# Softmax row sums of the long query chunks: from TensorE products with ones to sums on VectorE and one product per chunk

## The reference, cut to what matters

```python
paths = sigmoid(x @ Wp + bp)                       # 8 heads x 5 per token
agree = pq * pk + (1.0 - pq) * (1.0 - pk)
sim   = cumprod(agree, -1).sum(-1) / 5             # [head, query, key]
sim   = where(key > query, -inf, sim)
attn  = softmax(sim, -1)                           # exp / row sum over the keys
ctx   = attn @ V
x = layernorm(x + ctx @ Wo)
x = layernorm(x + (silu(x @ wg.T) * (x @ wu.T)) @ wd.T)
```

## Time and profile before

| | us |
|---|---|
| median of 3 runs | 887.72 (886.24 to 887.82) |
| the profiled execution, its own time | 885.52 |
| its span, first to last instruction | 883.8 |
| mean granted TensorE clock | 0.98 of full |

### The profile page before, as it was taken

The page is one execution under the profiler, slowest core; times in us unless marked ns, Lnnn a source line. Parts: engine busy times, 40 slices in busy tenths (PEclk is TensorE's granted clock), DMA queues, the critical chain, the costliest instruction groups (busy, mean ns, idle before and its releaser), DMA issues.

```text
span 883.8 us, 15437 instructions
## 1 busy us (share of the span) xinstructions
PE 832.1 (94%) x6146; PEld 412.3 (47%) x6146; DVE 481.5 (54%) x1021; ACT 454.1 (51%) x721; POOL 233.2 (26%) x266
## 2 busy tenths in 40 slices
PE   5299999999999999999999999999999999899986
PEld 3144355453644546454554536445364545344353
DVE  2934437645566545645376455665456553754466
ACT  2146654656456563656545564565636555364522
POOL 0011132223313232231322233132421313232224
PEclk9599999999999999999999999999999999999998
DMA  6750535005520336105360055303370062500001
GB/s 228 203 127 4 119 83 158 1 25 120 143 97 1 80 78 179 48 1 143 75 166 1 17 128 134 106 1 76 72 187 2 1 143 56 137 1 1 24 1 50
DMA packets 44362, 71.09 MB, mean 80 GB/s; under 512 B 3584, under 2 KB 21248, under 8 KB 44288
## 3 DMA queue, kind: packets, MB, share of 16 engines
q1 hardware_dynamic: 44288, 70.07, 30.1%
HBM read 53.28 MB, written 16.78 MB: 79 GB/s over the span
## 4 chain that ended last, share of the span: by engine, by line
PE 87%; DVE 6%; issue 2%; DMA 2%; ACT 1%; POOL 1%; SPq 1%; POOLq 0%; DVEq 0%; ACTq 0%
PE misc L821 17%; PE ctx_ps L786 16%; PE slot L764 15%; PE den_ps L786 13%; PE misc L833 9%; PE misc L740 7%; PE misc L798 6%; PE misc L749 2%; ACT probs L449 1%; DVE x1T_lo L600 1%; DMA query_stack<-phi_dram 1%; PE slot L821 1%; DVE ctx_raw L520 1%; PE misc L807 1%; DMA bp_sb<-in_bp_dram 1%
## 5 line engine op out<-in xcount | busy, mean ns | idle before, releaser
L449 ACT ACTIVATE probs<-slot 128x1024 f32<-128x1024 f32 (+3 forms) x384 | 290.1, 808 | 338.9 <-PE slot L764 338.6
L764 PE MATMUL slot<-query_stack,key_stack 128*128 128x512 f16 (+3 forms) x768 | 161.1, 331 | 16.3 <-DMA query_stack<-phi_dram 15.0
L786 PE MATMUL ctx_ps<-probs,vz_sb 128*32 128x512 f32 (+3 forms) x1536 | 164.5, 500 | 5.2 <-DVE ctx_raw L520 3.8
L402 POOL TENSOR_TENSOR work<-work 128x512 f16<-128x512 f32 x96 | 117.8, 1227 | 184.1 <-ACT work L467 184.1
L786 PE MATMUL den_ps<-probs,ones 128*32 128x512 f32 (+3 forms) x1536 | 159.6, 487 | 0.0
L388 POOL TENSOR_SCALAR_AFFINE_SELECT probs<-probs 128x512 f32<-128x512 f32 x128 | 82.0, 643 | 287.5 <-ACT probs L449 286.5
L821 PE MATMUL misc<-x1T_hi,w_parts 128*128 128x512 f16 x358 | 135.6, 379 | 6.3 <-DVE x1T_lo L600 6.0
L821 PE MATMUL misc<-x1T_lo,w_parts 128*128 128x512 f16 x358 | 135.7, 379 | 0.0
L610 DVE SCALAR_TENSOR_TENSOR work<-work,misc 128x512 f32<-128x512 f32 x89 | 61.1, 686 | 135.0 <-ACT work L461 135.0
L764 PEld LDWEIGHTS slot<-query_stack,key_stack 128*128 128x128 f16 x768 | 56.4, 98 | 167.5 <-issue 117.6
L833 PE MATMUL misc<-w_parts,work 128*128 128x256 bf16 x720 | 85.4, 276 | 3.9 <-POOL work L402 3.9
(11 more groups left out here) (74 smaller groups left out, 668.8 us busy)
## 6 DMA issues: line engine op xcount, KB each, us to landing
key_stack<-phi_dram SPq DMA_DIRECT2D x64, 256.0 KB, 5.7
query_stack<-phi_dram SPq DMA_DIRECT2D x64, 256.0 KB, 6.3
xT_sb<-in_xT_dram SPq DMA_DIRECT2D x8, 1024.0 KB, 5.0
x_sb<-in_x_dram SPq DMA_DIRECT2D x8, 1024.0 KB, 5.6
out_dram<-x SPq DMA_DIRECT2D x15, 512.0 KB, 3.5
phi_dram<-phi_hi SPq DMA_DIRECT2D x16, 256.0 KB, 2.1
phi_dram<-phi_lo SPq DMA_DIRECT2D x16, 256.0 KB, 2.4
work<-in_wgT_dram SPq DMA_DIRECT2D x1, 768.0 KB, 7.9
```

The source lines that it names most:

```text
L402: pool.tensor_tensor(hid_lo[:, n % M1, :], hid[:, n % HSLOTS, :], hid_hi[:, n % M1, :], ALU.subtract).then_inc(hid_lo_ready, 1)
L449: act.activation(probs[:, s % P_SLOTS, 2 * p:2 * p + 2, off:CH], slot[p][:, :, off:CH], ACT.Exp).then_inc(slot_drained[p], 1)
L764: mm = pe.matmul(slot[p][:, k, off:CH], key_stack[:, h, P * j:P * (j + 1)], query_stack[:, h, CH * c + off:CH * (c + 1)], start=True, stop ...
L786: mm = pe.matmul(sums[32 * k:32 * k + 32, off:CH], w, probs[:, s % P_SLOTS, k, off:CH], start=first, stop=final)
```

## The change

`ADD_FROM = {2: 3, 3: 1}`: in chunk 2 the steps of key tile 3 and later, in chunk 3 those of key tile 1 and later, are `ADDED`; those that come after the first of them are `ADDS`. In an added step `weigh` leaves out its four products with ones. In their place a new VectorE task `sum`, in the plan one step after the probabilities are made and ahead of that step's `BETWEEN` tasks, adds the four heads' probabilities (up to 128 x 2048, float32) into a new buffer `acc`; the first of a chunk adds two steps' probabilities. After the chunk's last `weigh`, four products of ones with `acc` go to `den_ps`. Five steps of chunk 2 (four adds) and seven of chunk 3 (six adds) are concerned. ScalarE waits for the add (`summed`) before it writes a ring buffer again, VectorE's `normalise` waits for `acc_used`.

```diff
+    ADD_FROM = {2: 3, 3: 1}
+    ADDED = [i for i, (q, c, g, j) in enumerate(STEPS) if q in ADD_FROM and j >= ADD_FROM[q]]
+    ADDS = [i for i in ADDED if STEPS[i][3] > ADD_FROM[STEPS[i][0]]]
+    NA = len(ADD_FROM)
...
-        return ([("weigh", b, NS - 3)] + gate_pair(b, 2) + [("weigh", b, NS - 2), ("weigh", b, NS - 1)] + halves(b, 2)
+        return ([("sum", b, NS - 1), ("weigh", b, NS - 3)] + gate_pair(b, 2) + [("weigh", b, NS - 2), ("weigh", b, NS - 1)] + halves(b, 2)
...
+        if s >= 1 and (s - 1) % NS in ADDS and s <= B * NS:
+            plan += [("sum", *divmod(s - 1, NS))]
         plan += between(b, i)
...
+        acc = sb("acc", [P, 4, CH], F32)
...
                 if s >= P_SLOTS:
                     act.wait_ge(pv_done, s - P_SLOTS + 1)
+                    b2, i2 = divmod(s - P_SLOTS, NS)
+                    if i2 in ADDED:
+
+                        i2 += i2 not in ADDS
+                        act.wait_ge(summed, len(ADDS) * b2 + ADDS.index(i2) + 1)
...
+            def add_up(b, i):
+
+                q, c, g, j = STEPS[i]
+                off = max(P * j - CH * c, 0)
+                s = NS * b + i
+                own = probs[:, s % P_SLOTS, :, off:CH]
+                count = len(ADDS) * b + ADDS.index(i)
+                if i in DIAG:
+                    dve.wait_ge(masked, len(DIAG) * b + DIAG.index(i) + 1)
+                else:
+                    for p in range(2):
+                        dve.wait_ge(slot_drained[p], s + 1)
+                if j == ADD_FROM[q] + 1:
+                    used = NA * b + list(ADD_FROM).index(q)
+                    if used:
+                        dve.wait_ge(acc_used, used)
+                    dve.tensor_tensor(acc[:, :, :], probs[:, (s - 1) % P_SLOTS, :, :], own, ALU.add).then_inc(summed, 1)
+                else:
+                    dve.wait_ge(summed, count)
+                    dve.tensor_tensor(acc[:, :, off:CH], acc[:, :, off:CH], own, ALU.add).then_inc(summed, 1)
...
                 dve.wait_ge(pv_done, NS * b + LAST[q] + 1)
+                if q in ADD_FROM:
+                    dve.wait_ge(acc_used, NA * b + list(ADD_FROM).index(q) + 1)
...
-                for sums, taken in ((ctx_ps, ctx_out), (den_ps, den_out)):
+                if first and NQ * b + q >= 1:
+                    pe.wait_ge(ctx_out, NQ * b + q)
+                for k in range(4):
+                    h = 4 * g + k
+                    mm = pe.matmul(ctx_ps[32 * k:32 * k + 32, off:CH], vz_sb[:, b % 2, j, 32 * h:32 * h + 32],
+                                   probs[:, s % P_SLOTS, k, off:CH], start=first, stop=final)
+                if i not in ADDED:
                     if first and NQ * b + q >= 1:
-                        pe.wait_ge(taken, NQ * b + q)
+                        pe.wait_ge(den_out, NQ * b + q)
                     for k in range(4):
-                        h = 4 * g + k
-                        w = vz_sb[:, b % 2, j, 32 * h:32 * h + 32] if taken is ctx_out else ones[:, :]
-                        mm = pe.matmul(sums[32 * k:32 * k + 32, off:CH], w,
+                        mm = pe.matmul(den_ps[32 * k:32 * k + 32, off:CH], ones[:, :],
                                        probs[:, s % P_SLOTS, k, off:CH], start=first, stop=final)
                 mm.then_inc(pv_done, 1)
+                if i in ADDED and final:
+                    pe.wait_ge(summed, len(ADDS) * b + ADDS.index(i) + 1)
+                    for k in range(4):
+                        mm = pe.matmul(den_ps[32 * k:32 * k + 32, :], ones[:, :], acc[:, k, :], start=False, stop=True)
+                    mm.then_inc(acc_used, 1)
```

More of the change, by code:

```diff
@@ L273, in seq_postln_kernel @@
         den_out = sem("den_out")
+        summed = sem("summed")
+        acc_used = sem("acc_used")
         den_recip_ready = sem("den_recip_ready")
@@ L695, in _ @@
                     split_weights()
+                elif what == "sum":
+                    add_up(*n)
                 elif what == "normalise":
```

## The result

| | before | after |
|---|---|---|
| median, us | 887.68 (886.24 to 887.82, 4 runs) | 862.49 (861.99 to 864.53, 4 runs) |
| ratio | | 0.972, 95% interval 0.9701 to 0.9739 |
| profiled execution, us | 885.52 | 864.53 |
| its span, us | 883.8 | 862.8 |
| a batch, us | 103.29 | 100.18 |

Faster by 25 us where 16 were forecast (872, range 850 to 885). The time lies inside the range, but 1.5 us under the forecast's own bounds (864 to 882). A second series of runs, beside the kernel before on the same chip, gave 862.31 and a ratio of 0.9739 (0.9717 to 0.9761), so 23 to 25 us. The two profiled executions differ by 21.0, because before's lies 2.2 under its median and after's 2.0 over it.

What follows compares the result with a forecast made beforehand. TensorE's work was taken as the bound. Per batch, 0.4 us (steps 13 to 15) plus 2.3 (19 to 23) minus 0.4 (the rest) gave 2.3, seven times 16: 869.5 profiled, 872 us median, range 850 to 885.

Steps and rivals of the forecast that it cites:

- The sum: Whole kernel: 2.3 us saved a batch, seven times, 16 us, giving a median of 872 us.
- the first rival: GpSimd's masks and subtracts hardly exclude VectorE's adds: 4.1 us saved a batch, about 858 us; chance 0.21.
- The bound and the removal: TensorE's work binds; leaving out products with ones takes 0.88 us off a 512-query step, net 6.2 us a batch.
- The adds: VectorE's new adds: 2.27 us for 2048 elements, 16.5 us a batch, VectorE busy about 613 us.
- The gate steps: Steps 19 to 23: add, mask and subtract take turns; 17.9 us after 20.19, saving 2.3 of 4.2 us.
- Steps 13 to 15: Chunk 2: TensorE waits about 2 us for a buffer behind VectorE's adds; 0.4 of 2.4 us stays saved.
- blocked mask: Steps 13 to 15: perhaps 0.6 us for a mask, counted in VectorE's 7.8 to 8.4 us.
- Steps 16, 17, 0 and 1: Steps 16 and 0 save 0.45 us each, 17 and 1 gain 0.88 less 0.23: together 0.4 us lost.
- The last batch: Chunk 3 saves nothing there, since TensorE's projection starts 0.26 us after the last `normalise`.
- The ring: ScalarE's wait before rewriting a probability buffer costs nothing as long as VectorE lags by less than a step.
- The slower rival: VectorE's queue in steps 19 to 23 and 13 to 14: nothing overlaps, 5.5 us a step, about 912 us; chance 0.16.
- The signs: Products with ones fall about 63 us; adds over 3 us behind mask or subtract; L402 and L388 well above 1.23 and 0.64.

Runs made afterwards that it cites:

- nearly no adds: The changed kernel with every add cut to the last 32 queries of each head: 841.99 us, ratio 0.9488.
- where GpSimd only writes: The changed kernel with GpSimd's mask and subtract replaced by constant writes, so GpSimd reads nothing in SBUF: 855.71 us, ratio 0.9644.
- chunk 3 alone: The change in chunk 3 only, with chunk 2 as in the kernel before: 871.89 us, ratio 0.9832 to the kernel before.
- all-late kernel: The changed kernel with every add moved behind the other VectorE tasks of its plan step: 901.47 us, ratio 1.016.
- two late kernels: The changed kernel with every add behind its plan step's other tasks, with three probability ring buffers (901.47 us) and with four (861.22 us).

## Why the prediction was right, and where it was off

The direction, the mechanism and the places of the waits were right; the sum was 9.5 us too slow. The forecast's own bounds (864 to 882) were missed by 1.5 us, and the range held because it took in the first rival as well.

- **The bound and the removal: right, a little too high.** 6.2 us a batch were counted from starts 0.88 us apart; four products are worth 0.85, and with nearly no adds 5.4 us arrive.
- **The adds: right.** 2.27 us estimated, 2.28 measured alone; VectorE 614 us busy for 613 to 615.
- **The gate steps: a mis-sized term.** "In a diagonal step (20 to 23) add, mask and subtract in turn are 2.27 + 0.64 + 1.16 = 4.07 us" led to 11.5 us for steps 20 to 22. They take 3.84 + 3.58 + 3.78 = 11.2, and 17.5 instead of 17.9 for steps 19 to 23. From one add's start to the next it is 3.58 and 3.78 us (509.50, 513.08, 516.86), because whole durations were added. A VectorE instruction begins 0.07 to 0.08 us before the one ahead has ended (add at 509.50, next at 511.71: 2.21 for 2.29), and mask and subtract together stick out over L648 and L656 by only 0.3 us. The rule that the prediction cites from the Trainium skill (SBUF — State Buffer, Who interferes with whom), that such pairs exclude each other, agrees with the trace but for 0.14 us: mask 2.11 us for 0.64 behind an add, add 2.48 for 2.28 behind a subtract, and neither where GpSimd only writes. The 0.14 is how much sooner the blocked one is done than its own time after the recorded end of the other: the subtract ends at 513.42 and the add at 515.56, 2.14 later; the mask ends 0.50 after the add.
- **Steps 13 to 15: right in kind, the other mis-sized term.** TensorE waits for L638 as said, 0.50 us, and before that 0.39 for L648 and L656, which wasn't forecast. The steps take 11.58 us, 0.85 less than the 12.43 of before, where 0.4 was forecast. The predicted blocked mask (0.6) fell on GpSimd instead (1.83 and 2.10 us in steps 13 and 14).
- **Steps 16, 17, 0 and 1: right.** Priced at 0.4 us lost, they lose 0.42 (5.03 to 4.59, 3.27 to 3.92, 4.59 to 4.16, 3.95 to 4.59). But the 0.65 of the product with `acc` in step 17 is not a cost that stands by itself: chunk 3 alone does without it and pays 0.62 in step 20.
- **The sum.** 3.1 us a batch came in place of 2.3, 0.45 of it from steps 13 to 15 and 0.37 from steps 19 to 23: some 5.7 us in seven batches. The last batch was forecast at zero for chunk 3, and chunk 2 was left out of it without a reason. From a feature copy of step 23 in the seventh batch to the end it is 142.95 us before and 141.68 after (140.8 in the second trace of the changed kernel), 1.3 to 2.2 us less. The 2 us or so that are left have no place of their own: two traces of the changed kernel differ by 2.6 us in their spans, 1.3 of it before the first feature copy.
- **The ring, costed at nothing "as long as VectorE lags by less than a step":** true for the changed order, and by little. In step 16 ScalarE's exponentials begin at 491.82, released by an add (L548) after 3.38 us idle, 0.72 us after the scores began at 491.10, and the step loses nothing by it (4.59 us, 4.60 with short adds). With the adds behind their step's tasks the same wait made the kernel slower than before. The slower rival had named VectorE's queue as the place, with mask and subtract in the way as its cause; the way that really leads there is this one.
- **The first rival (no exclusion, 858)** has its own run, with 855.7. The exclusion was priced at 13 us; it is worth 4.5 in the eight batches and, by the medians, at most 6.8 in all. The rival's step lengths were not met even so: without exclusion steps 20 to 22 take 3.85, 3.58 and 3.58 us, not 3.7, 3.7 and 3.2, since VectorE's own three instructions fill them.
- **The signs.** The products with ones fell by 63 us of group busy time as said (159.7 to 79.6, and 16.7 for those with `acc`). Two signs failed: the subtracts did not lengthen (1.21 us in the mean, 1.23 before), and full adds behind a subtract took 2.48 us, not over 3 (one of 16 did, with 3.25).

## What to carry to other kernels

When work moves from the engine that binds to one that has room, average room says little: go step by step, by the distance between starts and not by durations, and look whose buffer is read behind the new instruction. Put a long moved instruction behind the reads that another engine waits for, but only so far as the ring it reads from allows; an instruction that reads two ring buffers gives the older one back a step late, and between a ring of three and one of four that was 40 us here. Two engines that exclude each other cost only what can't hide beside other work of either (here 0.56 us of a batch of 100.18).

## What the runs showed that was not expected

- In the all-late kernel step 14 (2.48 us busy of 3.76) and a wait of TensorE of 1.28 us were followed by a stretch at a granted clock of 0.76, in which `down` took 3.87 us, where the changed kernel's takes 2.79. In steps 14 and 15 of the changed kernel (2.79 busy of 3.18, 4.42 of 4.92) the clock was 1.00. Over the whole execution the all-late kernel had a mean granted clock of 0.971, the changed one 0.980, so part of the 40 us between the two late kernels is clock.
- Held-back masks show up as long masks (2.11 us), not as idle time, so GpSimd's busy share rose from 26% to 34% without any new work: 61 us of waiting counted as work.
